# Second halves of the mixture dealt three parts later among the maxima

## What is computed

```
x = layernorm(x + attention(x))
x = layernorm(x + mixture(x))
```

```
h   = relu(flat @ shared_w1 + b1);  out  = flat + h @ shared_w2 + b2
hj  = relu(flat @ w1[j] + b1[j]);   out += gate[:, j] * (hj @ w2[j] + b2[j])
```

## Time and profile before

| what | value |
|---|---|
| median of three runs | 1475.87 us (1475.16 to 1476.57) |
| the profiled execution's own time | 1475.45 us |
| its span, first to last instruction | 1473.4 us |
| busy: PE, DVE, ACT, POOL | 91%, 74%, 57%, 36% |
| mean granted TensorE clock, of full | 0.958 |
| chain that ended last, by engine | PE 49%, DVE 25%, ACT 12%, issue 5% |
| 320 reductions of the maxima (L1351) | 378.7 us busy, 40.0 us idle before them |
| 2400 matmuls of `down` (L569) | 314.6 us busy |
| 1200 matmuls of `up` (L557) | 311.9 us busy |

### The profile page before, as it was taken

The page is one execution under the profiler, slowest core; times in us unless marked ns, Lnnn a source line. Parts: engine busy times, 40 slices in busy tenths (PEclk is TensorE's granted clock), DMA queues, the critical chain, the costliest instruction groups (busy, mean ns, idle before and its releaser), DMA issues.

```text
span 1473.4 us, 29057 instructions
## 1 busy us (share of the span) xinstructions
PE 1342.5 (91%) x10992; PEld 738.3 (50%) x10992; DVE 1092.0 (74%) x2747; ACT 840.4 (57%) x1266; POOL 532.7 (36%) x638
## 2 busy tenths in 40 slices
PE   5687999999998999989999999989999899999697
PEld 3322475436654366535654366543764347553364
DVE  6993688857897588966888578975789668885534
ACT  5406773396635875287733966358762777439221
POOL 3203542254323542245422543235422454225143
PEclk8757999999999999999999999999999999999799
DMA  6001032200221011210222002210212102220031
GB/s 240 16 14 16 15 87 67 52 18 21 95 66 37 30 61 62 67 31 16 86 67 52 19 21 93 68 35 30 59 59 70 32 16 67 72 51 16 16 112 60
DMA packets 52283, 77.81 MB, mean 53 GB/s; under 512 B 6334, under 2 KB 26800, under 8 KB 51888
## 3 DMA queue, kind: packets, MB, share of 16 engines
q1 hardware_dynamic: 52144, 75.96, 17.5%
HBM read 67.02 MB, written 8.65 MB: 51 GB/s over the span
## 4 chain that ended last, share of the span: by engine, by line
PE 49%; DVE 25%; ACT 12%; issue 5%; DVEq 4%; POOL 3%; DMA 2%; SPq 0%; POOLq 0%
PE PS L569 10%; PE PS L557 9%; PE PS L713 7%; ACT UQ L987 7%; DVE CM L1351 6%; DVE hr L1158 4%; PE PS L487 4%; PE PS L504 3%; POOL hp L1046 3%; ACT UK L987 2%; DVEq L1150 2%; PE PS L768 2%; PE PS L408 2%; PE PS L723 2%; DVE CM L1270 2%
## 5 line engine op out<-in xcount | busy, mean ns | idle before, releaser
L1046 POOL TENSOR_TENSOR hp<-hr,hp 128x512 f16<-128x512 f32 (+1 forms) x200 | 236.8, 1184 | 606.8 <-ACT hp L844 542.8
L1351 DVE TENSOR_REDUCE CM<-PS 128x32 f32<-128x1024 f32 x320 | 378.7, 1219 | 40.0 <-PE PS L487 36.0
L569 PE MATMUL PS<-W,hp 128*128 128x256 f16 (+1 forms) x2400 | 314.6, 274 | 18.7 <-POOL hp L1046 16.8
L557 PE MATMUL PS<-x1T,W 128*128 128x512 f16 (+1 forms) x1200 | 311.9, 387 | 0.0
L569 PEld LDWEIGHTS PS<-W,hp 128*128 128x128 f16 (+1 forms) x2400 | 214.3, 98 | 106.7 <-POOL hp L1046 44.2
L835 ACT ACTIVATE hr<-PS,CF 128x512 f32<-128x512 f32 (+1 forms) x200 | 136.9, 685 | 194.3 <-PE PS L557 189.1
L844 ACT ACTIVATE hp<-hr 128x512 f16<-128x512 f32 (+1 forms) x178 | 112.5, 632 | 232.8 <-DVE hr L1158 219.8
L1158 DVE TENSOR_TENSOR hr<-hr,gB 128x512 f32<-128x512 f32 x176 | 126.2, 717 | 67.7 <-ACT hr L835 61.7
L557 PEld LDWEIGHTS PS<-x1T,W 128*128 128x128 f16 (+1 forms) x1200 | 108.5, 100 | 113.1 <-issue 35.8
L987 ACT ACTIVATE UK<-PS 128x1024 f32<-128x1024 f32 x160 | 153.2, 1040 | 11.1 <-PE PS L504 10.7
L987 ACT ACTIVATE UQ<-PS 128x1024 f32<-128x1024 f32 x160 | 150.7, 1044 | 3.0 <-PE PS L504 1.5
(11 more groups left out here) (150 smaller groups left out, 1796.4 us busy)
## 6 DMA issues: line engine op xcount, KB each, us to landing
gB<-gates SPq DMA_DIRECT2D x64, 256.0 KB, 3.3
gB<-gates SPq DMA_DIRECT2D x32, 224.0 KB, 2.9
gB<-gates SPq DMA_DIRECT2D x32, 192.0 KB, 2.9
gB<-gates SPq DMA_DIRECT2D x32, 160.0 KB, 2.6
xT<-in_xT SPq DMA_DIRECT2D x8, 512.0 KB, 5.3
qET<-rows SPq DMA_DIRECT2D x16, 256.0 KB, 5.1
v<-in_x SPq DMA_DIRECT2D x8, 512.0 KB, 4.0
gB<-gates SPq DMA_DIRECT2D x32, 128.0 KB, 2.9
```

The costliest lines, as they stand in the source:

```text
L557: mm = pe.matmul(PS[0:w, BK_H[c % 2], :], W1[:, a, k, bass.ds(f0, w)], x1T[:, e, k, :], start=(n == 0), stop=(n == 5))
L569: mm = pe.matmul(PS[:, BK_Y + j // 2, (j % 2) * D:(j % 2 + 1) * D], hp[0:w, slot, a, j * P:(j + 1) * P], W2[0:w, e, bass.ds(c, 1), :].rear ...
L1046: nc.gpsimd.tensor_tensor(hp[0:w, slot, 1, :], hr[0:w, slot, :], hp[0:w, slot, 0, :], ALU.subtract).then_inc(pool_hp, 1)
L1351: nc.vector.tensor_reduce(dst, src, AX.X, ALU.max).then_inc(dve_cm, 1)
```

## The change

Three edits. The list `DEALT` is written out anew: instead of three parts of `up` of a chunk and then four of `down` of the one before, the two kinds alternate. In numbers of the list, `up` of chunk cc (from cc 1 on) stands at 7cc-3, 7cc-1 and 7cc+1, where it stood at 7cc to 7cc+2; `down` of the same chunk stands at 7cc+10, +12, +14 and +16, where it stood at 7cc+10 to +13. The entry of a `down` now bears its own chunk's number, and PE's call is written to match. On DVE `gated` goes by part 2 in place of part 3: by the last part of the chunk's own `up`.

```diff
-DEALT = [(c, part) for c in range(MC) for part in range(7)]
+DEALT = [(0, 0), (0, 1), (0, 2), (-1, 3)]
+for _c in range(1, MC):
+    DEALT += [(_c, 0), (_c - 2, 4), (_c, 1), (_c - 2, 5), (_c, 2), (_c - 2, 6), (_c - 1, 3)]
+DEALT += [(MC - 2, 4), (MC - 2, 5), (MC - 2, 6)]
...
-                                down(m, c - 1, (C_MAX[0] + cc - 1) % 2, part - 3)
+                                down(m, c, (C_MAX[0] + cc) % 2, part - 3)
...
                         for cc, part in dealt(u - 1) if m is not None and u else ():
-                            if part == 3:
+                            if part == 2:
                                 gated(m, i * MC + C_MAX[0] + cc, (C_MAX[0] + cc) % 2)
```

## The result

The changed kernel takes 1453.55 us (median of 4, 1452.11 to 1453.96) against 1475.51 for the kernel before beside it: 22.0 us less, ratio 0.9849, 95% interval 0.9836 to 0.9861. The profiled execution took 1453.75 us, its span is 1451.7.

What follows compares the result with a forecast made beforehand. The prediction took PE to set the pace, its waits passing on to DVE. Seven turns at 2.9 us less make 20.3, from 1475.45 to 1455.2 on the profiled execution, 1455.6 as median; range 1450 to 1465.

Steps and rivals of the forecast that it cites:

- PE's balance: PE's 55.71 us from first unit to end of last `max_unit`: 53.1 of work, about 2.5 of waits.
- step 1: `gated` one unit ahead for all 11 chunks gains one reduction, 1.14 us; all PE waits for `low` go.
- Steps 2 and 3: `gated` on DVE waiting for `relu`, cover 0.8; `high` on ACT waiting for `down` part 3, cover 1.7 us; cost nothing.
- Step 4: PE needs the selection's copies sooner: no wait for the first, 0.1 us for the second.
- Step 5: PE changes between `up` and `down` some 30 times more per turn: taken as 0, upper bound 0.3 us.
- Step 6: Stage's end: last `max_unit` 2.4 us earlier, DVE's own work allows it, L1360 of tile 0 2.5 us earlier.
- Step 7: `low` of chunk 21 meets L1360 of tile 0: 0.5 us lost each turn in place of 0.91 on tile 1.
- The sum: Whole kernel: seven turns, each 2.9 us shorter, 20.3 us less in all, giving 1455.6 us.
- that sign: Starts of the first reduction in successive turns were to come about 2.9 us closer.
- Rival A: Only PE's visible idle time in the stage comes back, 1.64 us per turn, 11.5 in all: 1464 us; chance 0.13.
- Rival B: The gain is all waited away at the end of the stage, where the attention starts: 1475 us; chance 0.08.
- Rival C: DVE waits in `gated` for a late `relu`, each lateness paid 77 times: slower, 1493 us; chance 0.09.

Runs made afterwards that it cites:

- Experiment 1: Kernel before with its old order of parts, only `gated` marked by part 2 in place of part 3: 1456.11 us, ratio 0.9869.
- experiment 2: Changed kernel's new order of parts on PE, but `gated` at the units where the kernel before had it: 1478.41 us, ratio 1.0021.
- experiment 6: Changed kernel with `gated` one reduction sooner still: ratio 0.9870, and run again for a trace 1458.03 us, ratio 0.9884.
- experiments 4 and 3: 4: changed kernel, `low` of chunk 21 writing 2 of 512 columns, 1451.31 us; 3: changed kernel, `gated` of chunk 21 behind the last reduction, 1456.96 us.

## Why the prediction was right, step by step

- **PE's balance and step 1** (2.5 us of waits for `low`, all gone). Right: 55.71 became 53.23, and no wait for `low` is left in the stage. Experiment 1 shows that the earlier `gated` does it, experiment 2 that the new order of the parts alone does not. One thing came out by luck: the waits for `low` are 2.27 by PE's starts, and the other 0.27 of the 2.5 are two for a reduction. I counted them as saved and gave no reason; the new deal did take them away (experiment 1 has both still, experiment 2 only the smaller).
- **Steps 2 and 3** (no new wait on DVE or on ACT). Right: in the changed kernel L1163 does not wait in the stage. What I wrote of the room, 0.8 us, fits experiment 6: one reduction less leaves waits of 0.2 to 0.4.
- **Step 4** (0.1 us for the selection's second copy). 0.12.
- **Step 5** (nothing for changing between `up` and `down`). Right: 0.34 in both orders.
- **Step 6** (DVE has the last two reductions early enough). Right: 53.06 from the first to the last start against 55.11. My own times give 53.2, 0.15 more; half of that is PE's part, which became 2.48 shorter and not 2.4. It is where the sum falls short of the measured 3.04.
- **Step 7** (`low` meets tile 0 for 0.5 in place of tile 1 for 0.91). 0.53 and 0.90; experiments 4 and 3 take either away or bring it back. "Each turn" was too much: in turn 4 the two are 0.17 and 0.56. And `low` ended 0.14 before tile 0's operation, as I took it, not 0.29.
- **The sum.** 2.9 per turn against 3.04 measured; 20.3 against 22.0 in all. The first reductions of successive turns came 3.1 closer on average, single ones 2.1 to 4.0, so that sign holds for the mean only. The part outside the seven stages is small, 0.4 of 21.7 in the profiled pair; which of it is clock I can't tell.
- **Rival A** (only the 1.64 us per turn that the windows call idle) falls: PE reads busy throughout now and the stage became 2.48 shorter, more than the idle time there was to lose. The modelled ends had filled gaps that were real.
- **Rival B** (given back at the end of the stage) falls: L1163 of chunk 22 is 3.04 earlier, and 3.1 arrives at the next turn.
- **Rival C's price was wrong**, though its case did not come. I had each late `relu` paid 77 times. Experiment 6 made it late by some 0.3, which would be 77 x 0.3 = 23 us, 3.3 per turn; it cost 1.4. Idle time that the reductions had anyway (1.1) paid for part, and five of eleven `gated` did not wait; that a wait in a ring makes a later one smaller is a guess that fits and is not shown.

## What to carry to other kernels

When PE waits for a product that goes through several engines, follow the way back to the first step that sits in another engine's queue for no reason of data: here `gated` stood behind one reduction too many, and to put it one place forward was worth nearly all of the change. Measure a stage between two instructions of one engine by their starts, not by busy shares: modelled ends hid up to 0.17 us of each wait here, and the shorter waits wholly. And look at what a moved instruction frees or meets further on: a fifth of this gain came from the last `gated` and from which VectorE operation the GpSimd one behind it hits.

## What the runs showed of the hardware

A VectorE operation with two inputs in SBUF that starts during `low` on GpSimd ends its own duration less 0.14 us after `low` does, whatever its size and however early it began. Three sizes show it: 0.28 after for the one of 0.42; 0.14 after for the one of 0.29 (451.13 + 0.82 = 451.95, `low` to 451.81); and 0.54 after for the one of 0.68, which is `gated` itself, at the next `low` of the changed kernel:

```profile
454.93 1.16 POOL L1051 TENSOR_TENSOR hp<-hr,hp 128x512 f16<-128x512 f32 x1 [3.12 <-ACT hp L849]
```
```profile
455.44 1.19 DVE L1163 TENSOR_TENSOR hr<-hr,gB 128x512 f32<-128x512 f32 x1 [0.16 <-issue]
```

It is the same within 0.01 in ten traces (before, after and eight of the experiments' runs), for 16 `gated` in each and for the 7 L1365 in each of the seven where `low` meets it. Turn 4 of the changed kernel shows that the start does not matter. There L1365 begins 0.36 later against `low` than in turn 2, takes 0.46 and not 0.82, and ends again 0.14 after it:

```profile
788.64 1.16 POOL L1051 TENSOR_TENSOR hp<-hr,hp 128x512 f16<-128x512 f32 x1 [4.16 <-ACT hp L849]
```
```profile
789.48 0.46 DVE L1365 SCALAR_TENSOR_TENSOR rep<-cbias,CM 128x128 f32<-128x128 f16 x1 [0.44 <-issue]
```

So the operation is shut out until shortly before the other's recorded end, and the price is the time from its start to that point. The prediction weighed two readings: what the Trainium skill says ("SBUF — State Buffer", "Who interferes with whom": an exclusive lock for the whole instruction), by which tile 0 would end 0.29 after `low`, and a little overlap, 0.15 after. Measured was 0.14. It is the Trainium skill's lock but for a fixed 0.14; whether GpSimd lets go that much early or its record runs that much long, no run here shows. The reductions, with their one input in PSUM, ran beside 11 such `low` per turn at 1.21 to 1.23 us each, untouched.
